# Stationary weights of an AdaLN mixture-of-experts feed-forward kernel stored in other forms

## The chip, the cores and the metric

The kernel runs on one core of one Trainium2 chip. The metric is device microseconds (us) from the start of the program to its end. Of the kernel before, two runs took 1309.41 and 1309.58 us, median 1309.49 us.

## The reference, cut to what matters

```python
B, S, D = (32, 256, 256); F, E, R, K = 1024, 8, 16, 2
# attention: q = x + bias of the sequence's stage, keys and values are the side input
attn = softmax(einsum('bsd,btd->bst', q, side));  o = einsum('bst,btd->bsd', attn, side)
# feed-forward with two of eight low-rank experts for each token
t = o * rsqrt(mean(o * o) + EPS) * norm_w
probs = softmax(t @ gate_w.T);  topw, topi = top_k(probs, K)
h1 = (t @ w1.T)[None] + SCALING * einsum('etr,efr->etf', einsum('td,erd->etr', t, a1), b1)
h3 = (t @ w3.T)[None] + SCALING * einsum('etr,efr->etf', einsum('td,erd->etr', t, a3), b3)
act = silu(h1) * h3
out_e = act @ w2.T + SCALING * einsum('etr,edr->etd', einsum('etf,erf->etr', act, a2), b2)
out = x + weighted sum of out_e over the token's two experts
```

## The kernel before, in words

All products are wanted in nearly float32 precision. Every operand is therefore stored as two tensors of the type float32r (a float32 that TensorE streams in one pass): a rounded high part `_hi`, and the rest, `_lo`. The helper `product` in the TensorE part makes one product out of three matmuls: high weight with high stream, high weight with low stream, low weight with high stream. In the profile these three are the lines L1201, L1202 and L1203, for every product of the kernel. For each matmul TensorE first loads a stationary operand of 128 columns (a row of the engine PEld), then streams the moving operand past it (a row of PE). A tile in the trace reads `bank<-t_hi,w1T_hi`: the moving operand is named first, the stationary one second.

The kernel has two phases. In the first, 32 sequences go through attention, one at a time; on TensorE there are 256-column products with q, k, prob and value, and 128-column transposes of q, kv and prob. Between them lie 21 "weight jobs" (the list `jobs`): a job transposes up to four 128x128 blocks of a weight into a PSUM bank (`weight_job`, L1247), ScalarE copies the bank into the high part (`weight_high`, L639), VectorE writes the low part (`weight_low`, L848). The weights of `w2` and `a2` arrive with the eight chunks interleaved, so the transposes of these jobs already load a stationary operand whose columns lie eight words (32 bytes) apart (`w2_in[:, c, j0 + k:F:FC]` and `a2_in[:, j0 + k:F:FC]`); those of `w1`, `w3` and `b` load packed columns.

In the second phase, 8192 tokens go through the feed-forward in 16 tiles of 512 tokens; in each tile a loop runs over 8 chunks j of 128 hidden features. `low_rank` multiplies with a13T; `first_expert` with w1T, b1T, w3T and b3T; `second_expert` with b1T and b3T; `down_z` with a2T. In all these the weight is stationary and 512 columns of tokens are streamed. `down_y` and `finish_y` are the other way round: the activation (s or z) is stationary and 256 columns of w2T or b2T are streamed. The order on TensorE is written out by hand in `pe_tile`. 

The stationary operand of a chunk is today a packed run of 128 words, 512 bytes. The allocations are laid out one behind the other, with pads: in the kernel before, all weights that are loaded as stationary, and t_hi, t_lo, v_hi, v_lo, s and br that are streamed or loaded in the second phase, start at the same place within a 512-byte grid (byte 384). The streamed kT, probT, w2T and b2T start at other places, by gaps of 8 to 88 words ahead of them.

Of the kernel before, what the change touches and what calls it, by code (L numbers as in the profile page):

```python
# [31 lines left out]
P = 128  # L32
# [20 lines left out]
def adaln_moe_ffn(nc, x, side, itok, embed, norm_w, w1, w3, w2, gate_w, a1, b1, a3, b3, a2, b2, out):  # L53
    ctx = ExitStack()
    with ctx:
# [6 lines left out]
        def sb(stack, name, shape, dt=F32):  # L62
            return stack.enter_context(nc.sbuf_tensor(name, shape, dt))
# [7 lines left out]

        sb(ctx, "pad_w", [P, 352])
        ident = sb(ctx, "ident", [P, P])
# [7 lines left out]

        w1T = split("w1T", [P, DC, F])
        w3T = split("w3T", [P, DC, F])
        w2T = split("w2T", [P, FC, D], gaps=(16, 24))
        a2T = split("a2T", [P, FC, ER], gaps=(88, 0))
# [35 lines left out]

        sb(ctx, "pad_t", [P, 48])
        O_STRIDE = P + 32
# [181 lines left out]
        for j0 in range(0, FC, 2):  # L305
            jobs.append(([(128 * (2 * k + c), 128, w2_in[:, c, j0 + k:F:FC], P)
                          for k in range(2) for c in range(DC)],
                         [(0, 512, w2T[0][:, j0:j0 + 2].rearrange("p j d -> p (j d)"),
                           w2T[1][:, j0:j0 + 2].rearrange("p j d -> p (j d)"), 1.0)]))
        B_JOB = len(jobs)  # L310
        for src, dst in ((b1_by_j, b1T), (b3_by_j, b3T)):
            for j0 in range(0, FC, 4):
                jobs.append(([(128 * k, 128, src[:, j0 + k].rearrange("p e r -> p (e r)"), P) for k in range(4)],
                             [(0, 512, dst[0][:, j0 * P:(j0 + 4) * P],
                               dst[1][:, j0 * P:(j0 + 4) * P], SCALING)]))
        A2_JOB = len(jobs)
        for j0 in range(0, FC, 4):
            jobs.append(([(128 * k, 128, a2_in[:, j0 + k:F:FC], ER) for k in range(4)],
                         [(0, 512, a2T[0][:, j0:j0 + 4].rearrange("p j e -> p (j e)"),
                           a2T[1][:, j0:j0 + 4].rearrange("p j e -> p (j e)"), 1.0)]))  # L320
        B2_JOB = len(jobs)
# [508 lines left out]
        def _(dve):  # L830
# [14 lines left out]
            def weight_low(n):  # L845
                dve.wait_ge(w_hi_ready, n + 1)
                for col, cols, hi, lo, scale in jobs[n][1]:
                    last = nc.vector.scalar_tensor_tensor(lo, job_bank(n)[:, col:col + cols], scale, f32(hi),  # L848
                                                          ALU.mult, ALU.subtract)
                last.then_inc(w_lo_ready, 1)  # L850
# [346 lines left out]
        def _(pe):  # L1197
# [188 lines left out]
            def first_expert(c, j):  # L1386
                f = slice(j * P, (j + 1) * P)
                for wT, bT, dst, k, done in ((w1T, b1T, h1_bank[j % 2], 0, h1_first),
                                             (w3T, b3T, h3_bank[j % 2], 1, h3_first)):
                    if j == 0:  # L1390
                        pe.wait_ge(v_ready, v_count(c, k + 2))
                    for dc in range(DC):
                        product(dst[:, :], at(wT, ALL, dc, f), (t_hi[c % 2][:, dc], t_lo[c % 2][:, dc]), dc == 0, False)
                    if j == 0:
                        pe.wait_ge(v_lo_ready, v_count(c, k))
                    product(dst[:, :], at(bT, ALL, f), (v_hi[k][:, :], v_lo[k][:, :]), False, True).then_inc(done, 1)

            def second_expert(c, j):
# [18 lines left out]
            def last_down_z(c, j):  # L1417
                (hi, lo), (s_high, s_low) = at(a2T, ALL, j), at(s_at(c, j), ALL, ALL)
                pe.wait_ge(last_br_ready, 1)
# [102 lines left out]
```

## Time and profile before

| | kernel before |
|---|---|
| median of the runs | 1309.49 us |
| the profiled execution, device time | 1309.57 us |
| its span from the first to the last instruction | 1307.7 us |
| TensorE matmul busy | 1300.9 us, 7278 instructions |
| TensorE weight load busy | 1138.8 us, 7278 instructions |
| VectorE, ScalarE, GpSimd busy | 844.1, 527.1, 250.0 us |
| granted TensorE clock | 1.000, all of the span |
| first phase, second phase | 0 to 179 us, 179 to 1307.7 us |

The profile is of one execution. Times in it are us, the mean duration of a group is ns. Matmul records overlap: the next one starts while the last one drains, and its end is modelled. How fast TensorE goes is read from start to start, in the timeline, and not from the durations. PE is a matmul, PEld a weight load. "x4" is four like instructions merged into one row.

### The profile page before, as it was taken

How to read it: one execution, taken by the hardware profiler on the slowest of the kernel's cores; microseconds unless marked ns; L12 is line 12 of the kernel's file. 1: busy time of each engine (PE TensorE's matmuls, PEld its weight loads, DVE VectorE, ACT ScalarE, POOL GpSimd, SP SyncE). 2: the span in 40 equal slices, each digit the busy share in tenths (PEclk: the TensorE clock that was granted, in tenths of full speed). 3: DMA queues.
4: the chain of work that ended last, by engine and by line, in shares of the span. 5: the costliest groups of instructions: out<-in, count | busy, mean ns of one | idle time of the engine just before them, and what ended most of it. 6: DMA issues, size and time to landing. Idle time of an engine off the chain costs nothing.

```text
span 1307.7 us, 18591 instructions
## 1 busy us (share of the span) xinstructions
PE 1300.9 (99%) x7278; PEld 1138.8 (87%) x7278; DVE 844.1 (65%) x1558; ACT 527.1 (40%) x991; POOL 250.0 (19%) x213
## 2 busy tenths in 40 slices
PE   9999999999999999999999999999999999999998
PEld 8999998888888888888888888888888888888887
DVE  6776656756666576656775567557675666565556
ACT  6776653333343334333333334333333343243332
POOL 2656640202011020202020202011020202020200
PEclk9999999999999999999999999999999999999999
DMA  9454811020202020101102020202020101102000
GB/s 287 140 159 147 233 50 33 2 73 1 73 2 73 1 73 1 58 17 28 46 2 73 1 73 2 73 1 73 2 73 1 57 17 34 41 1 73 1 17 17
DMA packets 73583, 69.56 MB, mean 53 GB/s; under 512 B 7050, under 2 KB 64792, under 8 KB 73368
## 3 DMA queue, kind: packets, MB, share of 16 engines
q1 hardware_dynamic: 72924, 68.11, 17.4%
q8 instruction: 57, 0.93, 0.3%
q10 hardware_dynamic: 572, 0.28, 0.1%
q14 instruction: 30, 0.25, 0.1%
HBM read 51.27 MB, written 17.10 MB: 52 GB/s over the span
## 4 chain that ended last, share of the span: by engine, by line
PE 98%; ACT 1%; DVE 1%; DMA 0%; issue 0%; ACTq 0%; DVEq 0%
PE bank L1202 31%; PE bank L1201 31%; PE bank L1203 31%; PE bank L1327 2%; PE bank L1254 2%; PE bank L1305 1%; PE bank L1247 1%; DMA kv<-in_fside_BxSxS 0%; ACT prob L662 0%; PE bank L1292 0%; ACT kT_hi L646 0%; ACT qT_hi L645 0%; DVE q L858 0%; DVE x_out L1145 0%; PE bank L1334 0%
## 5 line engine op out<-in xcount | busy, mean ns | idle before, releaser
L1073 DVE TENSOR_TENSOR act_a<-silu_a,bank 128x512 f32<-128x512 f32 x128 | 87.6, 685 | 211.2 <-PE bank L1203 194.6
L753 ACT ACTIVATE br_hi<-act_br 128x512 fp32r<-128x512 f32 x128 | 80.9, 632 | 188.5 <-DVE act_br L1084 188.5
L746 ACT ACTIVATE silu_b<-bank 128x512 f32<-128x512 f32 x128 | 76.2, 596 | 187.9 <-PE bank L1203 187.1
L589 POOL TENSOR_TENSOR t_lo<-t_in,t_hi 128x512 fp32r<-128x512 f32 x32 | 40.6, 1290 | 552.2 <-ACT t_hi L733 552.2
L1202 PE MATMUL bank<-w2T_lo,s_hi 128*128 128x256 f32 x512 | 144.7, 283 | 0.0
L1203 PE MATMUL bank<-w2T_hi,s_lo 128*128 128x256 f32 x512 | 143.3, 280 | 0.0
L1201 PE MATMUL bank<-w2T_hi,s_hi 128*128 128x256 f32 x512 | 142.7, 279 | 0.0
L1081 DVE TENSOR_TENSOR act_b<-silu_b,bank 128x512 f32<-128x512 f32 x128 | 87.9, 687 | 81.4 <-PE bank L1203 80.3
L742 ACT ACTIVATE silu_a<-bank 128x512 f32<-128x512 f32 x128 | 75.7, 591 | 134.3 <-PE bank L1203 134.2
L608 POOL TENSOR_TENSOR v_lo<-v_full,v_hi 128x512 fp32r<-128x512 f32 x64 | 94.5, 1511 | 136.7 <-ACT v_hi L738 136.7
L1094 DVE TENSOR_TENSOR br_lo<-act_br,br_hi 128x512 fp32r<-128x512 f32 x128 | 104.7, 818 | 5.6 <-ACT br_hi L753 3.1
L1088 DVE TENSOR_TENSOR act_s<-act_a,act_br 128x512 f32<-128x512 f32 x128 | 103.2, 806 | 4.4
L1201 PE MATMUL bank<-t_hi,w1T_hi 128*128 128x512 f32 x256 | 100.4, 392 | 0.0
L1084 DVE TENSOR_TENSOR act_br<-act_b,rho 128x512 f32<-128x512 f32 x128 | 97.2, 760 | 4.4
L1203 PE MATMUL bank<-t_hi,w1T_lo 128*128 128x512 f32 x256 | 99.9, 390 | 0.0
L1201 PE MATMUL bank<-v_hi,b1T_hi 128*128 128x512 f32 x256 | 99.8, 390 | 0.0
L1202 PE MATMUL bank<-t_lo,w1T_hi 128*128 128x512 f32 x256 | 99.7, 390 | 0.0
L1202 PE MATMUL bank<-v_lo,b1T_hi 128*128 128x512 f32 x256 | 99.7, 390 | 0.0
L1201 PE MATMUL bank<-v_hi,b3T_hi 128*128 128x512 f32 x256 | 99.7, 389 | 0.0
L1202 PE MATMUL bank<-v_lo,b3T_hi 128*128 128x512 f32 x256 | 99.6, 389 | 0.0
L1203 PE MATMUL bank<-v_hi,b1T_lo 128*128 128x512 f32 x256 | 99.6, 389 | 0.0
L1201 PE MATMUL bank<-t_hi,w3T_hi 128*128 128x512 f32 x256 | 99.6, 389 | 0.0
(197 smaller groups left out, 3242.4 us busy)
## 6 DMA issues: line engine op xcount, KB each, us to landing
x_in<-in_x SPq DMA_DIRECT2D x32, 256.0 KB, 3.7
t_scratch<-oT SPq DMA_DIRECT2D x32, 256.0 KB, 2.5
t_in<-t_scratch SPq DMA_DIRECT2D x16, 512.0 KB
x_out<-in_x SPq DMA_DIRECT2D x16, 512.0 KB, 3.9
kv<-in_fside_BxSxS SPq DMA_DIRECT2D x31, 256.0 KB, 3.4
out<-x_out SPq DMA_DIRECT2D x30, 256.0 KB, 4.0
rho<-scale_scratch SPq DMA_DIRECT2D x16, 256.0 KB
rstd<-scale_scratch SPq DMA_DIRECT2D x16, 256.0 KB
```

The source lines that it names most:

```text
L608: nc.gpsimd.tensor_tensor(v_lo[k][:, :], v_full[k][:, :], f32(v_hi[k][:, :]), ALU.subtract).then_inc(v_lo_ready, 1)
L742: nc.scalar.activation(silu_a[j % 2][:, :], h1_bank[j % 2][:, :], ACT.Silu).then_inc(silu_a_ready, 1)
L746: nc.scalar.activation(silu_b[:, :], h1_bank[j % 2][:, :], ACT.Silu).then_inc(silu_b_ready, 1)
L753: nc.scalar.activation(br_hi[j % 2][:, :], act_br[j % 2][:, :], ACT.Copy).then_inc(br_hi_ready, 1)
L1073: nc.vector.tensor_tensor(act_a[j % 2][:, :], silu_a[j % 2][:, :], h3_bank[j % 2][:, :], ALU.mult).then_inc(act_a_ready, 1)
L1081: nc.vector.tensor_tensor(act_b[:, :], silu_b[:, :], h3_bank[j % 2][:, :], ALU.mult).then_inc(act_b_ready, 1)
L1084: nc.vector.tensor_tensor(act_br[j % 2][:, :], act_b[:, :], rho[c % 2][:, :], ALU.mult).then_inc(act_br_ready, 1)
L1088: nc.vector.tensor_tensor(act_s[j % 2][:, :], act_a[j % 2][:, :], act_br[j % 2][:, :], ALU.add).then_inc(act_s_ready, 1)
L1094: low = nc.vector.tensor_tensor(br_lo[j % 2][:, :], act_br[j % 2][:, :], f32(br_hi[j % 2][:, :]), ALU.subtract)
L1201: nc.tensor.matmul(dst, w_hi, x_hi, start=start, stop=False, skip_group_check=not grouped)
L1202: nc.tensor.matmul(dst, w_hi, x_lo, start=False, stop=False, skip_group_check=not grouped)
L1203: return nc.tensor.matmul(dst, w_lo, x_hi, start=False, stop=stop, skip_group_check=not grouped)
```

## The change

The change stores the stationary weights of the second phase in other forms, and leaves every instruction of TensorE in its place, with its shape.

- w1T: the high and low parts are interleaved word by word in one tensor `w1T_pair`, so the columns of each lie 8 bytes apart.
- a2T: four chunks are interleaved; columns 16 bytes apart.
- b1T: eight chunks are interleaved; columns 32 bytes apart.
- w3T and b3T stay packed, but begin 16 and 8 bytes (w3T high, low), 4 and 12 bytes (b3T high, low) off the 32-byte grid.
- w2T, the streamed weight, keeps its 256 packed words for each chunk, with 8 words (32 bytes) of room behind each. The weight jobs of w2T then write two pieces of 256 columns where they wrote one of 512.
- Pads and gaps are changed so that all other tensors keep their place within the 512-byte grid.

```diff
+        w1T_pair = sb(ctx, "w1T_pair", [P, DC, F, 2], F32R)
+        w1T = tuple(w1T_pair[:, :, :, k] for k in range(2))
+        w3T_hi = moved("w3T_hi", 4, DC * F)
+        sb(ctx, "w3T_gap", [P, 120])
+        w3T_lo = moved("w3T_lo", 2, DC * F)
+        w3T = tuple(part.rearrange("p (c f) -> p c f", c=DC) for part in (w3T_hi, w3T_lo))
+        w2T_rows = split("w2T", [P, FC, D + 8], gaps=(8, 0))
+        w2T = tuple(part[:, :, 0:D] for part in w2T_rows)
+        a2T_rows = split("a2T", [P, FC // 4, ER, 4], gaps=(112, 0))
+        a2T = tuple(part[:, :, :, :].rearrange("p f e i -> p f i e") for part in a2T_rows)
         a13T = split("a13T", [P, DC, 2, ER])
-        b1T = split("b1T", [ER, F])
-        b3T = split("b3T", [ER, F])
-        b2T = split("b2T", [ER, D], gaps=(72, 32))
+        b1T_rows = split("b1T", [ER, P, FC])
+        b1T = tuple(part[:, :, :].rearrange("p c f -> p f c") for part in b1T_rows)
+        b3T_hi = moved("b3T_hi", 1, F)
+        sb(ctx, "b3T_gap", [P, 120])
+        b3T_lo = moved("b3T_lo", 3, F)
+        b3T = b3T_hi, b3T_lo
+        b2T = split("b2T", [ER, D], gaps=(64, 32))
...
-                         [(0, 512, w2T[0][:, j0:j0 + 2].rearrange("p j d -> p (j d)"),
-                           w2T[1][:, j0:j0 + 2].rearrange("p j d -> p (j d)"), 1.0)]))
+                         [(256 * k, 256, w2T[0][:, j0 + k], w2T[1][:, j0 + k], 1.0) for k in range(2)]))
...
-                    last = nc.scalar.activation(hi, job_bank(n)[:, col:col + cols], ACT.Copy, scale=scale)
+                    last = nc.scalar.activation(hi, shaped(job_bank(n)[:, col:col + cols], hi), ACT.Copy, scale=scale)
```

Here `moved(name, words, n)` takes a tensor of n + 8 words and gives n words of it, beginning `words` words in.

On TensorE the order is the same row for row. This is the start of `first_expert` in the first tile, where the first chunk is multiplied with w1T and b1T. Before:

```order
L1201 MATMUL bank<-t_hi,w1T_hi 128x512
L1202 MATMUL bank<-t_lo,w1T_hi 128x512
L1203 MATMUL bank<-t_hi,w1T_lo 128x512
L1201 MATMUL bank<-t_hi,w1T_hi 128x512
L1202 MATMUL bank<-t_lo,w1T_hi 128x512
L1203 MATMUL bank<-t_hi,w1T_lo 128x512
L1201 MATMUL bank<-v_hi,b1T_hi 128x512
```

And in the change, at the same place:

```order
L1217 MATMUL bank<-t_hi,w1T_pair 128x512
L1218 MATMUL bank<-t_lo,w1T_pair 128x512
L1219 MATMUL bank<-t_hi,w1T_pair 128x512
L1217 MATMUL bank<-t_hi,w1T_pair 128x512
L1218 MATMUL bank<-t_lo,w1T_pair 128x512
L1219 MATMUL bank<-t_hi,w1T_pair 128x512
L1217 MATMUL bank<-v_hi,b1T_hi 128x512
```

Nothing moved; the source lines are 16 further down, and high and low weight of w1T have one tensor's name.

On ScalarE, in the first phase, the four jobs of w2T stand between the copies of attention. Before:

```order
L646 ACTIVATE kT_hi<-bank 128x512
L639 ACTIVATE w2T_hi<-bank 128x512
L662 ACTIVATE prob,row_sum<-bank,neg_max 128x256 x2
L656 ACTIVATE value_hi<-kv 128x512
L675 ACTIVATE oT<-bank 128x4x128
```

In the change:

```order
L662 ACTIVATE kT_hi<-bank 128x512
L655 ACTIVATE w2T_hi<-bank 128x256 x2
L678 ACTIVATE prob,row_sum<-bank,neg_max 128x256 x2
L672 ACTIVATE value_hi<-kv 128x512
L691 ACTIVATE oT<-bank 128x4x128
```

One ACTIVATE of 512 columns has become two of 256, four times; the same holds for the low parts on VectorE. GpSimd and the DMA queue have the same rows as before.

## Rows read from the trace of the kernel before

**Rows 1.** The page: span, busy time of the engines, granted clock.
```profile
span 1307.7 us, 18591 instructions
PE 1300.9 (99%) x7278; PEld 1138.8 (87%) x7278; DVE 844.1 (65%) x1558; ACT 527.1 (40%) x991; POOL 250.0 (19%) x213
PEclk9999999999999999999999999999999999999999
```

**Rows 2.** The page: the chain that ended last, by engine.
```profile
PE 98%; ACT 1%; DVE 1%; DMA 0%; issue 0%; ACTq 0%; DVEq 0%
```

**Rows 3.** Windows: stretch, then PE, PEld, DVE, ACT, POOL busy, granted clock.
```profile
8.00:66.00 58.00, 56.59 (x476) 55.70 (x476) 43.08 (x101) 42.86 (x106) 28.73 (x31) 1.00 0.71 216
...
700.00:1280.00 580.00, 580.00 (x2994) 497.67 (x2994) 367.60 (x599) 205.09 (x345) 78.36 (x56) 1.00 0.10 30
```

**Rows 4.** Matmul groups by form: line, tile, shapes, count | busy us, mean ns.
```profile
L1202 PE MATMUL bank<-w2T_lo,s_hi 128*128 128x256 f32 x512 | 144.7, 283 | 0.0
...
L1201 PE MATMUL bank<-t_hi,w1T_hi 128*128 128x512 f32 x256 | 100.4, 392 | 0.0
...
L1201 PE MATMUL bank<-br_hi,a2T_hi 128*128 128x512 f32 x128 | 49.8, 389 | 0.0
...
L1202 PE MATMUL bank<-probT_lo,value_hi 128*128 128x256 f32 x128 | 35.9, 280 | 0.0
L1327 PE MATMUL bank<-oT 128*128 128x136 f32 x256 | 34.9, 279 | 0.0
```

**Rows 5.** Timeline of PE from 699.83 us: start, duration, line, tile.
```profile
699.83 0.28 PE L1202 MATMUL bank<-w2T_lo,s_hi 128*128 128x256 f32 x1
...
702.07 0.28 PE L1203 MATMUL bank<-w2T_hi,s_lo 128*128 128x256 f32 x1
...
704.50 0.39 PE L1202 MATMUL bank<-t_lo,w3T_hi 128*128 128x512 f32 x1
...
711.98 0.39 PE L1202 MATMUL bank<-t_lo,w3T_hi 128*128 128x512 f32 x1
```

**Rows 6.** Timeline of PEld, weight loads of the same stretch.
```profile
701.96 0.19 PEld L1203 LDWEIGHTS bank<-w2T_hi,s_lo 128*128 128x128 f32 x1
...
704.50 0.19 PEld L1203 LDWEIGHTS bank<-t_hi,w3T_lo 128*128 128x128 f32 x1
```

**Rows 7.** Weight load groups: count | busy us, mean ns.
```profile
L1201 PEld LDWEIGHTS bank<-v_hi,b1T_hi 128*128 128x128 f32 x256 | 48.1, 188 | 9.5
...
L1327 PEld LDWEIGHTS bank<-oT 128*128 128x128 f32 x256 | 32.0, 190 | 0.2
```

**Rows 8.** Timeline of PE in the first phase: transposes of packed and spaced columns, then oT.
```profile
34.25 0.60 PE L1254 MATMUL bank<-ident,kv 128*128 128x128 f32 x4
34.68 0.60 PE L1247 MATMUL bank<-ident,w_in 128*128 128x128 f32 x4
35.12 1.09 PE L1327 MATMUL bank<-oT 128*128 128x136 f32 x8
```

**Rows 9.** Weight loads of L1247: duration ns least, median, most; first and last start.
```profile
L1247 PEld LDWEIGHTS bank<-ident,w_in x48: 139/140/193, 11.5 to 44.1; 128*128 128x128 f32 x48
L1247 PEld LDWEIGHTS bank<-ident,a_in x12: 185/189/230, 6.7 to 62.0; 128*128 128x128 f32 x12
```

**Rows 10.** Timeline of weight loads: first a w3 job (packed), then a w2 job (spaced).
```profile
31.84 0.47 PEld L1247 LDWEIGHTS bank<-ident,w_in 128*128 128x128 f32 x4
...
34.58 0.51 PEld L1247 LDWEIGHTS bank<-ident,w_in 128*128 128x128 f32 x4
```

**Rows 11.** ScalarE's part of the weight jobs: duration ns least, median, most.
```profile
L639 ACT ACTIVATE w2T_hi<-bank x4: 605/622/646, 35.9 to 44.7; 128x512 fp32r<-128x512 f32 x4
...
L639 ACT ACTIVATE b2T_hi<-bank x1: 393/393/393, 65.7 to 65.7; 128x256 fp32r<-128x256 f32 x1
```

**Rows 12.** The same on VectorE.
```profile
L848 DVE SCALAR_TENSOR_TENSOR w2T_lo<-bank,w2T_hi x4: 679/680/681, 36.7 to 45.5; 128x512 fp32r<-128x512 f32 x4
...
L848 DVE SCALAR_TENSOR_TENSOR b2T_lo<-bank,b2T_hi x1: 412/412/412, 66.5 to 66.5; 128x256 fp32r<-128x256 f32 x1
```

More of the change, by code:

```diff
@@ L80, in split, with moved @@
             return tuple(parts)
[L82 to L85, printed above, removed]
-        a13T = split("a13T", [P, DC, 2, ER])
-        b1T = split("b1T", [ER, F])
-        b3T = split("b3T", [ER, F])
-        b2T = split("b2T", [ER, D], gaps=(72, 32))
+        def moved(name, words, n):
+            room = sb(ctx, name, [P, n + 8], F32R)
+            return room[:, words:words + n]
+        w1T_pair = sb(ctx, "w1T_pair", [P, DC, F, 2], F32R)
[8 more added lines that the diff above has]
+        a2T = tuple(part[:, :, :, :].rearrange("p f e i -> p f i e") for part in a2T_rows)
+        a13T = split("a13T", [P, DC, 2, ER])
+        b1T_rows = split("b1T", [ER, P, FC])
[5 more added lines that the diff above has]
+        b2T = split("b2T", [ER, D], gaps=(64, 32))
         sb(ctx, "pad_b2T", [P, 24])
@@ L312, in adaln_moe_ffn @@
             for j0 in range(0, FC, 4):
-                jobs.append(([(128 * k, 128, src[:, j0 + k].rearrange("p e r -> p (e r)"), P) for k in range(4)],
-                             [(0, 512, dst[0][:, j0 * P:(j0 + 4) * P],
-                               dst[1][:, j0 * P:(j0 + 4) * P], SCALING)]))
+                places = ([(0, 512, dst[0][:, j0:j0 + 4], dst[1][:, j0:j0 + 4], SCALING)]
+                          if dst is b1T else [(0, 512, dst[0][:, j0 * P:(j0 + 4) * P],
+                                               dst[1][:, j0 * P:(j0 + 4) * P], SCALING)])
+                jobs.append(([(128 * k, 128, src[:, j0 + k].rearrange("p e r -> p (e r)"), P) for k in range(4)], places))
         A2_JOB = len(jobs)
@@ L318, in adaln_moe_ffn @@
             jobs.append(([(128 * k, 128, a2_in[:, j0 + k:F:FC], ER) for k in range(4)],
[L319 to L320 removed]
+                         [(0, 512, a2T[0][:, j0 // 4], a2T[1][:, j0 // 4], 1.0)]))
         B2_JOB = len(jobs)
@@ L847, in weight_low @@
                 for col, cols, hi, lo, scale in jobs[n][1]:
-                    last = nc.vector.scalar_tensor_tensor(lo, job_bank(n)[:, col:col + cols], scale, f32(hi),
+                    last = nc.vector.scalar_tensor_tensor(lo, shaped(job_bank(n)[:, col:col + cols], lo), scale, f32(hi),
                                                           ALU.mult, ALU.subtract)
@@ L1395, in first_expert @@
                         pe.wait_ge(v_lo_ready, v_count(c, k))
-                    product(dst[:, :], at(bT, ALL, f), (v_hi[k][:, :], v_lo[k][:, :]), False, True).then_inc(done, 1)
+                    product(dst[:, :], at(bT, ALL, j if bT is b1T else f), (v_hi[k][:, :], v_lo[k][:, :]), False, True).then_inc(done, 1)
             def second_expert(c, j):
@@ L1417, in last_down_z @@
             def last_down_z(c, j):
-                (hi, lo), (s_high, s_low) = at(a2T, ALL, j), at(s_at(c, j), ALL, ALL)
+                (hi, lo), (s_high, s_low) = at(a2T, ALL, j // 4, j % 4), at(s_at(c, j), ALL, ALL)
                 pe.wait_ge(last_br_ready, 1)
```

12 lines of the change are left out of this document (7 added, 5 removed).

## The prediction

> **What bounds the kernel now.** I read the page first. TensorE's matmuls are busy for 1300.9 of 1307.7 us, the granted clock is at its upper level (2.4 GHz) in every slice [rows 1], and 98% of the chain that ended last lies on TensorE [rows 2]. In the second phase there is no gap in it at all: 580.00 of 580.00 us, with VectorE at 63% and ScalarE at 35% [rows 3]. So only what changes the pace of TensorE's stream counts.
>
> Busy time does not show that pace, since matmul records overlap; start-to-start times do. From the matmul at 704.50 us to the one at 711.98 us there are 33 steps of 512 columns, all with a new weight: 7.48 / 33 = 0.2267 us each [rows 5]. The stream alone, 512 columns at 2.4 GHz, would take 0.2133 us. Each 512-column matmul thus costs 13.4 ns more than its stream. The 256-column matmuls from 699.83 to 702.07 us are 19 steps in 2.24 us, 0.118 us each against 0.107 us of stream: 11 ns more [rows 5]. The excess goes with the matmul, not with its length.
>
> How much room has the weight load? It starts together with the matmul before its own: load and matmul both at 704.50 us [rows 5, 6]. Its record is 188 ns long [rows 7]. In the 256-column stretch the load for the matmul at 702.07 starts at 701.96 us, yet that matmul starts 0.11 us later, though the record runs to 702.15 [rows 5, 6]. So the last 70 ns or so of a record hold nobody up, and a load needs at most 118 ns of its engine. In the 512-column stretch there are 227 ns. The slack is at least 227 - 118 = 109 ns for each load.
>
> **The change, part by part.** The profiled execution took 1309.57 us, of which 1307.7 are the span and 1.9 lie around it; the median of the runs is 1309.49, the same within 0.1 us.
>
> *Columns 8, 16, 32 bytes apart (w1T, a2T, b1T).* Each pair of a high and a low weight makes three matmuls: 3 x 256 with w1T, 3 x 256 with b1T, 6 x 128 with a2T [rows 4, 7], 768 for each of the three and 2304 together. What does a spaced load cost? The trace has them: the transposes of the w2 and a2 jobs load columns 32 bytes apart. Packed, such a load takes 140 ns (the median of all w_in), spaced up to 193, and a2's a_in have a median of 189 [rows 9]; four in a row take 0.51 instead of 0.47 us [rows 10]. So spacing costs a transpose's load about 50 ns. An ordinary load takes 188 ns packed [rows 7], as much as a spaced transpose load. I see two bounds. Below: 0, if the 188 ns is already the pace of one column at a time, which spacing doesn't alter; I take this one, since 187 to 193 ns and 188 ns are the same pace. Above: +53 ns, to 241 ns. Of that bound 118 + 53 = 171 ns count, still under 227. Either way the load stays hidden under the matmul before it, and the cost is 2304 x 0 = 0. The cover would be gone only if a load's own part grew past 227 ns, almost twice its 118.
>
> *w3T and b3T, 4 to 16 bytes off the grid.* These are 2 x 768 = 1536 loads under 512-column streams, and they stay packed. No row shows such a start; the nearest is that of packed loads, 188 ns [rows 7]. A run of 128 words that begins off the grid can touch at most one piece more of the memory than on it, 1 part in 32 of 118 ns, 4 ns, against a slack of 109. Cost 0.
>
> *w2T, 32 bytes further from chunk to chunk.* This is a streamed operand, and its 1536 matmuls of 256 columns run at 0.118 us [rows 4, 5]. Now each chunk begins at another place in the 512-byte grid. The trace of before has several such places: w2T_lo, 283 ns, and probT_lo, 280 ns, start 40 and 32 to 112 words off the stationary grid and last the same within 3 ns [rows 4]. I take 0, and 3 ns x 1536 = 4.6 us either way as bounds.
>
> *Jobs of the first phase.* ScalarE writes w2T_hi in two pieces: 2 x 393 instead of 622 ns, +0.16 us for each of four jobs [rows 11]; VectorE 2 x 412 instead of 680, +0.14 [rows 12]. Uncovered that is 4 x 0.30 = 1.2 us. It is covered: from 8 to 66 us ScalarE and VectorE have 15 us free each, and TensorE waits 1.4 us in all [rows 3]. Eight jobs (w1T, b1T, a2T) now write with spaced columns. No row prices that. If it doubled ScalarE's and VectorE's part (0.62 + 0.68 us) and nothing covered it, it would be 8 x 1.3 = 10 us; since both engines have room for all of it, I take 0, and 2 us as the upper bound.
>
> Sum: 1309.5 + 0 + 0 + 0 + 0 = about 1310 us, with a range of its own of 1303 to 1317.
>
> The Trainium skill, in "SBUF — State Buffer", section "Door 1: The DMA port swizzle", says that memory lines are 16 bytes, that two accesses to a line are needed for full bandwidth and that each step to a new line pays a penalty. By that w1T would be free, and b1T and a2T would not. The trace bears out that spacing costs a transpose's load something. If the penalty stays under the slack, the page and my sum give the same time; the two rivals that follow are what it gives if not.
>
> **Rival 1, slower: a load's reads take turns from the stream.** The 13.4 ns are 32 periods of 2.4 GHz, and 32 is a quarter of the load's 128 columns: as if each four packed columns stopped the stream once. Speaking for it: the eight oT matmuls stream 136 columns at half the pace (113.3 ns) with the same 190 ns loads [rows 7], and go (1.09 - 0.28) / 7 = 0.116 us from start to start [rows 8], only 2.7 ns over their stream. Where the stream leaves every second turn free, the load disturbs it little; where it takes every turn, 13.4 ns. Against it: the excess could as well belong to each column loaded, or be a fixed price of changing weights at full pace. The spaced transposes cannot decide, since their stream leaves turns free too: a w2 job goes from 34.68 to 35.12 us, 0.44 us, the packed kv before it from 34.25 to 34.68, 0.43 [rows 8]. If it holds, columns 8 bytes apart stop the stream 64 times (+13.3 ns), 16 and 32 bytes apart 128 times (+40 ns each): 768 x (13.3 + 40 + 40) = 71.7 us, 1381 us. It decides as soon as an additional stop costs more than a third of what it does today.
>
> The Trainium skill speaks against this rival: "TensorE: Matmul & The Clock Gate", section "Step-by-step: what each phase is for", says that the stream and the weight load have independent read ports and that loading steals no read bandwidth from a running matmul.
>
> **Rival 2: spaced loads become longer than their cover.** Doubling the 118 ns for a2T and b1T gives 236, 9 ns over 227: 1536 x 9 = 14 us, 1324 us, within 2%. Tripling gives 354, 127 ns over: 195 us, 1505 us. Against it: the 193 ns of rows 9.
>
> **Rival 3, faster: the spacing keeps load and stream out of each other's way.** If the 13.4 ns come from both readers meeting in the same part of the memory, a load with 8 bytes a column walks at another pace than today, and may meet the stream less. Down to the 2.7 ns of oT that gives 10.7 ns a matmul: for the 2304 spaced ones 24.7 us, 1285 us; with w3T and b3T (3840 in all) 41 us, 1268 us. Against it: the excess is 11 to 13 ns wherever the streams begin.
>
> **How the numbers follow.** The forecast gets 0.50. Rival 1 gets 0.20, as the oT rows are good evidence for half of it. Rival 2 gets 0.12, half within 2% and half beyond. Rival 3 gets 0.18, 0.11 of it beyond 2%, if the off-grid weights gain as well or the gain per matmul is larger. About 2% is what a measurement of this kernel can tell from no change. Faster 0.11, same 0.50 + 0.06 + 0.07 = 0.63, slower 0.20 + 0.06 = 0.26. The range from 1284 to 1382 us leaves out 0.11 below and 0.06 above.
>
> **What the profile would show.** Right: steps of 0.227 us between 512-column matmuls for all weights, loads of 188 to 241 ns, 580.00 busy of 580. Rival 1: 0.240 us after the start of a matmul during which a w1T weight is loaded, 0.267 for a2T and b1T, w3T and b3T as before. Rival 2: loads of a2T and b1T near 300 ns and TensorE paced by them. Rival 3: steps below 0.227 us. Gaps of TensorE between 30 and 66 us would show my cover for the jobs wrong.

## The result, and the profile after

The change takes 1341.69 us (1340.58 and 1342.81, median of two), before 1309.49. The ratio is 1.0248, with a 95% interval of 1.0231 to 1.0264: 32.2 us slower. That is within the stated range of 1284 to 1382 us, but 32 us off the likeliest case and outside the 1303 to 1317 us of the sum itself. The range reached this far for the sake of rival 1, whose sizes turned out wrong; that the time fell inside is owed to the width of the range and not to the sum.

| | before | after |
|---|---|---|
| median of the runs | 1309.49 us | 1341.69 us |
| span of the profiled execution | 1307.7 us | 1341.0 us |
| weight load busy | 1138.8 us | 1223.2 us |
| first phase ends | 179.1 us | 181.2 us |
| mean step after a 512-column matmul, second phase | 227.3 ns | 235.0 ns |
| mean step after a 256-column matmul, second phase | 118.2 ns | 118.3 ns |

The steps are my count over all matmuls of the second phase, from the start of one to the start of the next. 4032 steps of 512 columns, each 7.7 ns longer, are 31.0 us. The profiled execution is the longer of the two, 33.2 us over the profiled one of before (1342.81 against 1309.57 us); nearly all the rest is a first phase that ends 2.1 us later. Of the page of the profile, which [rows 1, 2] show of before:

```profile
span 1341.0 us, 18599 instructions
PE 1332.1 (99%) x7278; PEld 1223.2 (91%) x7278; DVE 846.8 (63%) x1562; ACT 532.0 (40%) x995; POOL 250.0 (19%) x213
...
PE 96%; ACT 2%; DMA 1%; DVE 1%; SPq 0%; issue 0%; DVEq 0%
```

TensorE's share says nothing: 99% before and after. The windows (stretch; then PE, PEld, DVE, ACT, POOL busy; granted clock), to be held against [rows 3]:

```profile
8.00:66.00 58.00, 54.53 (x457) 52.26 (x458) 43.04 (x102) 43.94 (x106) 27.72 (x30) 1.00 0.67 207
700.00:1280.00 580.00, 580.00 (x2913) 527.06 (x2912) 360.70 (x589) 201.52 (x337) 78.33 (x56) 1.00 0.11 34
```

In the second phase TensorE is still busy for 580.00 of 580.00 us at the full clock (its upper level, 2.4 GHz), but gets 2913 matmuls done where it did 2994. The weight loads fill 527 us of it instead of 498. The load groups (count | busy us, mean ns of one | idle of the load unit just before them), to be held against 188 ns and 9.5 us of idle time in [rows 7]:

```profile
L1218 PEld LDWEIGHTS bank<-v_lo,b1T_hi 128*128 128x128 f32 x256 | 84.8, 331 | 0.0
L1219 PEld LDWEIGHTS bank<-v_hi,b1T_lo 128*128 128x128 f32 x256 | 84.2, 329 | 0.0
...
L1217 PEld LDWEIGHTS bank<-t_hi,w1T_pair 128*128 128x128 f32 x256 | 49.7, 194 | 5.8
...
L1217 PEld LDWEIGHTS bank<-t_hi,w3T_hi 128*128 128x128 f32 x256 | 49.0, 191 | 5.4
...
L1219 PEld LDWEIGHTS bank<-t_hi,w3T_lo 128*128 128x128 f32 x256 | 48.0, 188 | 11.1
L1218 PEld LDWEIGHTS bank<-br_lo,a2T_hi 128*128 128x128 f32 x128 | 39.6, 310 | 0.0
```

Three kinds stand here. Columns 8 bytes apart cost a load 6 ns. Columns 16 and 32 bytes apart cost it 121 to 143 ns, and within a series its unit has no idle time left ahead of it. (Records of over 0.3 us that start every 0.24 us overlap, so an idle time of 0.0 does not yet say that a matmul waited.) The off-grid w3T stays at 188 to 191.

Next, PE's timeline, first and last matmul of each run of steps (start, duration), and the weight loads of the same stretch:

```profile
705.81 0.53 PE L1217 MATMUL bank<-v_hi,b1T_hi 128*128 128x512 f32 x1
706.18 0.40 PE L1218 MATMUL bank<-v_lo,b1T_hi 128*128 128x512 f32 x1
...
707.12 0.39 PE L1219 MATMUL bank<-v_hi,b3T_lo 128*128 128x512 f32 x1
...
708.53 0.39 PE L1219 MATMUL bank<-br_hi,a2T_lo 128*128 128x512 f32 x1
...
709.92 0.40 PE L1219 MATMUL bank<-t_hi,w1T_pair 128*128 128x512 f32 x1
...
710.64 0.40 PE L1219 MATMUL bank<-v_hi,b1T_lo 128*128 128x512 f32 x1
...
712.03 0.40 PE L1219 MATMUL bank<-t_hi,w3T_lo 128*128 128x512 f32 x1
```

```profile
705.70 0.32 PEld L1217 LDWEIGHTS bank<-v_hi,b1T_hi 128*128 128x128 f32 x1
...
709.92 0.32 PEld L1217 LDWEIGHTS bank<-v_hi,b1T_hi 128*128 128x128 f32 x1
710.16 0.33 PEld L1218 LDWEIGHTS bank<-v_lo,b1T_hi 128*128 128x128 f32 x1
710.40 0.33 PEld L1219 LDWEIGHTS bank<-v_hi,b1T_lo 128*128 128x128 f32 x1
710.65 0.19 PEld L1217 LDWEIGHTS bank<-t_hi,w3T_hi 128*128 128x128 f32 x1
```

Read against the 0.2267 us of [rows 5], all with 512 columns:

- six steps from 707.12 to 708.53 us, a2T being loaded: 0.235 us each;
- six from 708.53 to 709.92, w1T loaded: 0.232;
- three from 709.92 to 710.64, b1T loaded: 0.240. The loads follow each other at 0.24, 0.24 and 0.25 us as well. Each starts with a matmul, so these times alone do not tell which of the two waits for the other;
- six from 710.64 to 712.03, w3T loaded: 0.232, although these loads are as short as before.

At 705.81 a step takes 0.37 us. The b1T load of 0.32 us starts at 705.70 under a 256-column matmul, which covers only 0.12 of it. There are 15 such steps, one for each tile behind `finish_y`: 15 x (0.367 - 0.227) = 2.1 us.

These steps show that a long load does hold TensorE up, and where the wait is booked. The record of the matmul begins at 705.81 us, before its own load ends at 706.02, and is 0.53 us long: the wait stands in the step that begins with the matmul that uses the load. They also give an estimate of the part of a load that holds TensorE up: cover plus long step less a stream, 0.116 + 0.367 - 0.227, about 255 ns for the first load of b1T here. In the kernels below with b1T alone, the same 15 steps are 361 ns at 32 bytes and 343 ns at 16 (counted in their traces), which gives 255 and 235 ns.

By weight loaded, over the whole second phase: the mean step in ns, without the steps over 0.3 us. "Loaded" is the weight whose load starts with the step, which the next matmul uses. The experiments of the last seven columns follow below: b1T 8, 16, 32 bytes apart; a2T 16; the off-grid w3T and b3T; the same two packed at other places; and the change with b1T packed.

| loaded | before | change | b1 8 B | b1 16 B | b1 32 B | a2 16 B | off-grid | places | change, b1T packed |
|---|---|---|---|---|---|---|---|---|---|
| w1T high, low | 228.4, 227.5 | 232.0, 233.1 | 228.4, 227.5 | 228.4, 227.5 | 228.4, 227.5 | 229.0, 232.5 | 228.9, 228.3 | 229.2, 228.3 | 232.4, 233.0 |
| a2T high | 226.7 | 234.4 | 226.7 | 228.6 | 227.9 | 234.8 | 231.9 | 227.4 | 236.8 |
| a2T low | 226.7 | 235.1 | 226.7 | 229.3 | 230.0 | 235.8 | 228.1 | 227.9 | 234.3 |
| b1T high | 227.4 | 240.3 | 232.0 | 235.2 | 237.7 | 226.8 | 229.4 | 228.9 | 231.2 |
| b1T low | 227.3 | 245.4 | 233.2 | 233.2 | 248.1 | 227.2 | 230.5 | 228.8 | 230.5 |
| w3T high | 226.7 | 233.4 | 229.2 | 230.5 | 232.9 | 226.7 | 229.0 | 232.1 | 228.9 |
| w3T low | 226.7 | 227.5 | 226.7 | 233.3 | 233.6 | 226.7 | 227.1 | 228.8 | 227.1 |
| b3T high | 226.9 | 234.5 | 229.2 | 229.3 | 233.3 | 226.9 | 232.3 | 231.7 | 232.3 |
| b3T low | 226.9 | 231.7 | 226.7 | 231.3 | 232.3 | 226.9 | 229.4 | 231.2 | 229.4 |

High weights are loaded about 512 times, low ones 256. The additions for the change are therefore, in us: w1T 3.1, a2T 6.0, b1T 10.9 and the 2.1 of the 15 long steps, w3T 3.7, b3T 5.1; together 30.9. The rows of w3T and b3T are the surprise: 8.8 us with loads of 188 to 192 ns. A small part of it is b1T's, since the wait for its last load stands one step further on. Counted by the weight that the step's own matmul uses, the same trace gives w1T 3.7, a2T 6.0, b1T 14.2 (the long steps included), w3T 2.8 and b3T 4.5 us: 7.3 of the 8.8 us stay with w3T and b3T.

The weight jobs, to be held against [rows 11, 12] (duration least, median, most; first and last start):

```profile
L655 ACT ACTIVATE w2T_hi<-bank x8: 390/423/451, 37.0 to 46.2; 128x256 fp32r<-128x256 f32 x8
L655 ACT ACTIVATE w1T_pair<-bank,nw x4: 725/742/772, 14.2 to 19.8; 128x512 fp32r<-128x512 f32 x4
L655 ACT ACTIVATE w3T_hi<-bank,nw x4: 696/715/732, 22.9 to 33.9; 128x512 fp32r<-128x512 f32 x4
...
L655 ACT ACTIVATE b1T_hi<-bank x2: 1197/1222/1247, 49.1 to 52.4; 128x512 fp32r<-128x512 f32 x2
L655 ACT ACTIVATE b3T_hi<-bank x2: 610/628/645, 55.5 to 58.4; 128x512 fp32r<-128x512 f32 x2
L655 ACT ACTIVATE a2T_hi<-bank x2: 1117/1134/1152, 61.5 to 64.7; 128x512 fp32r<-128x512 f32 x2
```

```profile
L864 DVE SCALAR_TENSOR_TENSOR b1T_lo<-bank,b1T_hi x2: 1123/1136/1148, 50.3 to 53.7; 128x512 fp32r<-128x512 f32 x2
L864 DVE SCALAR_TENSOR_TENSOR b3T_lo<-bank,b3T_hi x2: 681/682/683, 56.5 to 59.1; 128x512 fp32r<-128x512 f32 x2
L864 DVE SCALAR_TENSOR_TENSOR a2T_lo<-bank,a2T_hi x2: 1108/1113/1118, 62.6 to 65.9; 128x512 fp32r<-128x512 f32 x2
```

Writes 8 bytes apart are nearly free (742 against 715 ns). Those 16 and 32 bytes apart take nearly double: b1T 1222 against 628 for the packed b3T, and 1136 against 682 on VectorE, which also reads the spaced high part.

TensorE is busy 54.53 of the 58 us of this stretch, 56.59 before. Of these 2.1 us, 1.6 lie before 30 us, where TensorE waits mostly for data to arrive (0.89 us for kv, 0.59 for w_in) and for q. Between 30 and 66 us, where the prediction wanted to see no gap, TensorE is busy for 35.57 of 36.00 us, before for all 36.00: the cover of the jobs leaks 0.4 us. In the last three kernels below, which keep at least six of the eight spaced jobs, that leak is 0.2 to 0.4 us and the second phase begins between 179.0 and 179.3 us; one of them keeps all eight and the split w2T jobs too, and begins it at 179.0. So I don't count the later start of this one execution as a cost of the change.

### The profile page after: what moved, and what is told of

Same layout as the page of the kernel before. It is cut to its first block, busy times and chain, and to the rows that moved or that the text cites. A ratio compares the mean times of both kernels' runs of the same rounds, so it can differ in the third digit from the quotient of the medians.

```text
span 1341.0 us, 18599 instructions
## 1 busy us (share of the span) xinstructions
PE 1332.1 (99%) x7278; PEld 1223.2 (91%) x7278; DVE 846.8 (63%) x1562; ACT 532.0 (40%) x995; POOL 250.0 (19%) x213
## 4 chain that ended last, share of the span: by engine, by line
PE 96%; ACT 2%; DMA 1%; DVE 1%; SPq 0%; issue 0%; DVEq 0%
PE bank L1217 30%; PE bank L1219 30%; PE bank L1218 30%; PE bank L1270 2%; PE bank L1343 2%; PE bank L1321 1%; ACT prob L678 1%; DMA x_in<-in_x 0%; DMA kv<-in_fside_BxSxS 0%; PE bank L1263 0%; ACT qT_hi L661 0%; ACT kT_hi L662 0%; DVE q L874 0%; SPq L411 0%; SPq L460 0%
## 5 line engine op out<-in xcount | busy, mean ns | idle before, releaser
L1217 PE MATMUL bank<-v_hi,b1T_hi 128*128 128x512 f32 x256 | 106.1, 415 | 0.0
L1218 PE MATMUL bank<-v_lo,b1T_hi 128*128 128x512 f32 x256 | 104.7, 409 | 0.0
L1219 PE MATMUL bank<-v_hi,b1T_lo 128*128 128x512 f32 x256 | 102.9, 402 | 0.0
L1219 PE MATMUL bank<-v_hi,b3T_lo 128*128 128x512 f32 x256 | 101.6, 397 | 0.0
L1219 PE MATMUL bank<-t_hi,w1T_pair 128*128 128x512 f32 x256 | 101.2, 395 | 0.0
L1219 PE MATMUL bank<-t_hi,w3T_lo 128*128 128x512 f32 x256 | 101.0, 394 | 0.0
L1217 PE MATMUL bank<-t_hi,w1T_pair 128*128 128x512 f32 x256 | 100.8, 394 | 0.0
L1218 PE MATMUL bank<-t_lo,w1T_pair 128*128 128x512 f32 x256 | 100.8, 394 | 0.0
```

The lines of the kernel that those rows point to most:

```text
L1217: nc.tensor.matmul(dst, w_hi, x_hi, start=start, stop=False, skip_group_check=not grouped)
L1218: nc.tensor.matmul(dst, w_hi, x_lo, start=False, stop=False, skip_group_check=not grouped)
L1219: return nc.tensor.matmul(dst, w_lo, x_hi, start=False, stop=stop, skip_group_check=not grouped)
```

## The experiments

Two theories are weighed. One is that of cover: a spaced load grows longer than the matmul above it, and only then costs. The other is that of disturbance: a load disturbs the running stream by how or where it reads, though it is itself in time. Every ratio is against the kernel before, run on the same chip. The source lines shift by some rows from kernel to kernel.

### w1T alone, 8 bytes apart

```diff
-        w1T = split("w1T", [P, DC, F])
+        w1T_pair = sb(ctx, "w1T_pair", [P, DC, F, 2], F32R)
+        w1T = tuple(w1T_pair[:, :, :, k] for k in range(2))
```

> Only w1T has its columns 8 bytes apart; all else is the kernel before. Theory A (a load that is spaced too far becomes long, and TensorE waits for it where the matmul before it does not cover it): in the changed kernel w1T's loads took 194 ns against 188, so they stay covered; time 1309 to 1311 us, and steps of about 227 to 228 ns. Theory B (a load's reads take turns from the stream, by the number of pieces of memory that it touches): twice the pieces, +5 to +13 ns for each of the 768 matmuls under which w1T is loaded, +4 to +10 us, 1314 to 1320 us, with the load's record no longer than before.

Measured: 1313.72 against 1308.97 us, ratio 1.0034 [1.0022, 1.0047], +4.8 us. One load group, and PE's timeline with six steps ahead of which w1T is loaded:

```profile
L1202 PEld LDWEIGHTS bank<-t_hi,w1T_pair 128*128 128x128 f32 x256 | 49.7, 194 | 8.7
```

```profile
710.60 0.39 PE L1204 MATMUL bank<-br_hi,a2T_lo 128*128 128x512 f32 x1
...
712.00 0.40 PE L1204 MATMUL bank<-t_hi,w1T_pair 128*128 128x512 f32 x1
```

The load is 6 ns longer and has idle time ahead of it (8.7 us over 256), yet each of the six steps takes 0.233 us, 6 ns more. The load is not late. Cover alone can't explain this; the result lies between the two expectations. In this form w1T high still begins at its old place and w1T low 4 bytes behind it, and both have mean steps of 233 ns (232.7 and 232.9), so it is the spacing that costs here and not those 4 bytes.

### a2T alone, 16 bytes apart

```diff
-        a2T = split("a2T", [P, FC, ER], gaps=(88, 0))
+        a2T_rows = split("a2T", [P, FC // 4, ER, 4], gaps=(88, 0))
+        a2T = tuple(part[:, :, :, :].rearrange("p f e i -> p f i e") for part in a2T_rows)
```

> Only a2T has its columns 16 bytes apart. In the changed kernel its loads took 309 ns against 188. Theory A: the load's own part is about 118 + 121 = 239 ns, 12 ns over the 227 of its cover, for 768 loads, +9 us, 1318 us; the steps are all near 239 ns, set by the load. Theory B: stops of the stream that come on top of its own pace, +40 ns by the count of pieces, +31 us, 1340 us. The sum by weight in the changed kernel's trace gave +6 us for a2T; I expect 1315 to 1319 us.

Measured: 1317.50 against 1308.97 us, 1.0064 [1.0049, 1.0079], +8.5 us.

```profile
L1205 PEld LDWEIGHTS bank<-br_lo,a2T_hi 128*128 128x128 f32 x128 | 39.6, 309 | 0.0
```

The load goes from 188 to 309 ns, with no idle time left. By the arithmetic of the prediction its own part is 118 + 121 = 239 ns, 12 over the 227 of the stream; the steps are 231 to 240 ns long, mean 235 to 236. In the mean, cover says what happens, and the 235 ns from the long steps above agree. It does not say it step by step: the six steps of a series are 231, 240, 232, 238, 231 and 240 ns, where the expectation had all of them near 239. And 1.3 us of the loss lies in steps under which the untouched w1T low is loaded (232.5 instead of 227.5 ns).

### b1T alone, 32 bytes apart

```diff
-        b1T = split("b1T", [ER, F])
+        b1T_rows = split("b1T", [ER, P, FC])
+        b1T = tuple(part[:, :, :].rearrange("p c f -> p f c") for part in b1T_rows)
```

> Only b1T has its columns 32 bytes apart. In the changed kernel its loads took 317 to 331 ns. Theory A: its own part is about 118 + 135 = 253 ns, up to 26 ns over the cover, less where a stop of the stream isn't needed: +11 to +20 us for 768 loads, and once a tile, behind the 256-column matmuls of finish_y, a step of 367 ns in which the cover is only 118 ns (15 times, 2 us); 1322 to 1331 us. Theory B: +31 us, 1340 us, the same as for a2T, since both touch one piece for each column.

Measured: 1332.85 against 1308.97 us, 1.0180 [1.0165, 1.0195], +23.9 us. Load group, then PE's timeline:

```profile
L1208 PEld LDWEIGHTS bank<-v_hi,b1T_lo 128*128 128x128 f32 x256 | 85.2, 333 | 0.0
```

```profile
704.39 0.40 PE L1208 MATMUL bank<-t_hi,w1T_lo 128*128 128x512 f32 x1
...
705.11 0.41 PE L1208 MATMUL bank<-v_hi,b1T_lo 128*128 128x512 f32 x1
...
705.83 0.39 PE L1208 MATMUL bank<-t_hi,w3T_lo 128*128 128x512 f32 x1
...
706.51 0.39 PE L1208 MATMUL bank<-t_hi,w3T_lo 128*128 128x512 f32 x1
...
707.19 0.40 PE L1208 MATMUL bank<-v_hi,b3T_lo 128*128 128x512 f32 x1
```

The three steps from 704.39 with b1T loaded take 0.240 us. Then the first three with the *unchanged* w3T loaded take 0.240 each as well (249, 236 and 235 ns), and from 705.83 on the steps are back at 0.227. The 249 ns are still the wait for the last load of b1T, booked one step on; the two behind it are slow although the loads are 188 to 192 ns long. So something is handed on. How far differs from place to place: over the 128 times that w3T follows b1T, its six steps have means of 243, 235, 236, 226, 229 and 231 ns. With columns 16 bytes apart the trail is longer and even: 230, 231, 236, 228, 232 and 231 ns behind b1T, 224, 231, 236, 228, 232 and 231 behind a2T, and then 227. Nor does the load ahead have to be late: in the kernel with w1T alone the two steps behind w1T's 194 ns loads are 233 and 231 ns, with packed b1T loaded. By the table, 4.9 + 4.7 = 9.6 of the 23.9 us lie in the steps of w3T and b3T; counted by the weight that the step's own matmul uses, 5.8.

### w3T and b3T alone, 4 to 16 bytes off the grid

```diff
-        w3T = split("w3T", [P, DC, F])
+        w3T_hi = moved("w3T_hi", 4, DC * F)
+        sb(ctx, "w3T_gap", [P, 120])
+        w3T_lo = moved("w3T_lo", 2, DC * F)
...
+        b3T_hi = moved("b3T_hi", 1, F)
+        sb(ctx, "b3T_gap", [P, 120])
+        b3T_lo = moved("b3T_lo", 3, F)
```

> Only w3T (16 and 8 bytes) and b3T (4 and 12 bytes) are off the 32-byte grid. In the changed kernel the steps while these were loaded were 227.5 to 234 ns, which may be delay handed on from the long loads of b1T and a2T, or their own. If it is handed on (theory A alone): 1309 to 1311 us and steps of 227 ns. If a start off the grid, or a start at another place than the stream's, itself costs something: +3 to +7 ns for 1536 loads, +5 to +9 us, 1314 to 1319 us, and then by load: w3T low (8 bytes) nothing, the other three 4 to 6 ns.

Measured: 1319.30 against 1308.97 us, 1.0078 [1.0063, 1.0093], +10.3 us, with loads like this:

```profile
L1213 PEld LDWEIGHTS bank<-t_hi,w3T_hi 128*128 128x128 f32 x256 | 48.1, 188 | 10.2
```

The load records are unchanged within 1 ns, and yet 10 us. This is disturbance without any lack of cover. The time is at the upper end of the second expectation, but its sizes by load are not borne out: w3T high rises by 2.3 ns, w3T low by 0.4, b3T high by 5.4 and b3T low by 2.5. Over half of the loss lies in the steps of weights that were not touched, a2T high (231.9 ns) and b1T (229.4 and 230.5) above all.

### b1T 8 bytes apart, and 16

```diff
+        b1T_pair = sb(ctx, "b1T_pair", [ER, FC, P, 2], F32R)
+        b1T = tuple(b1T_pair[:, :, :, k] for k in range(2))
```

> Only b1T is changed, to columns 8 bytes apart (high and low word by word, as w1T is in the change). w1T alone with 8 bytes cost 4.8 us for 768 loads (steps of 233 ns), with loads of 194 ns. If the price goes with the spacing and not with the weight: +4 to +7 us, 1313 to 1316 us, loads of 194 ns, and no 367 ns steps behind finish_y. If b1T is dear for its place in the order, whatever its spacing: over +12 us.

```diff
+        b1T_rows = split("b1T", [ER, FC // 4, P, 4])
+        b1T = tuple(part[:, :, :, :].rearrange("p a c i -> p a i c") for part in b1T_rows)
```

> Only b1T is changed, to columns 16 bytes apart, as a2T is in the change. a2T alone with 16 bytes cost 8.5 us (loads 309 ns), b1T alone with 32 bytes 23.9 us (loads 317 to 342 ns). If the length of the load decides: loads of 309 ns, steps of 230 to 240 ns, +8 to +12 us with about 2 us of it behind finish_y, 1317 to 1321 us. If one piece of memory for each column is what costs, 16 and 32 bytes are the same: about +24 us, 1333 us.

Measured, against 1309.28 us: 8 bytes apart 1315.04, 1.0043 [1.0027, 1.0059], +5.8; 16 bytes apart 1324.32, 1.0113 [1.0095, 1.0131], +15.0. A load group of the kernel with 8 bytes:

```profile
L1206 PEld LDWEIGHTS bank<-v_hi,b1T_pair 128*128 128x128 f32 x256 | 49.7, 194 | 9.4
```

And one of the kernel with 16:

```profile
L1207 PEld LDWEIGHTS bank<-v_lo,b1T_hi 128*128 128x128 f32 x256 | 79.6, 311 | 0.0
```

With one weight, the loads are 188 ns packed, 194 at 8 bytes, up to 311 at 16, up to 333 at 32. The jump lies between 8 and 16. The Trainium skill, "SBUF — State Buffer", section "Door 1: The DMA port swizzle", has memory lines of 16 bytes, with two accesses to a line for the full rate and a penalty for each new line; the trace agrees for weight loads on where the jump lies, with these four numbers. By that rule 16 and 32 bytes, both with one column to a line, would be alike; the further 22 ns are not in it. The 15 long steps are there at 16 bytes (0.343 us) and at 32 (0.361) and not at 8 (0.234). The whole program pays 0, 5.8, 15.0 and 23.9 us. The 5.8 are as expected; the 15.0 lie above the one expectation and below the other. Nor does the length of the load decide alone: a2T with the same 16 bytes and the same 309 ns cost 8.5 us. b1T is loaded in 256 groups of three, a2T in 128 groups of six, and behind a group come the six slow steps seen above; in the trace with b1T 16 bytes apart 7.6 us lie in the steps of the untouched w3T, b3T and a2T.

### w3T and b3T packed, on the 32-byte grid, at other places

Compared with the kernel before, w3T high and low are moved by 32 and 64 bytes, b3T high and low by 128 and 256; all four remain multiples of 32 bytes.

```diff
+        w3T_hi = moved("w3T_hi", 8, DC * F)
+        w3T_lo = moved("w3T_lo", 16, DC * F)
...
+        b3T_hi = moved("b3T_hi", 32, F)
+        b3T_lo = moved("b3T_lo", 64, F)
```

> The kernel before, with w3T and b3T packed and on the 32-byte grid, but off their place within 512 bytes: w3T high by 32, low by 64 bytes, b3T high by 128, low by 256. The off-grid kernel (4 to 16 bytes) cost 10.3 us. If it is the start inside a 32-byte piece that costs: this one is 1309 us with steps of 227 ns. If it is any shift of the load against the stream (the streams start at byte 384 as the weights did): +5 to +15 us, 1314 to 1324 us, with steps while w3T and b3T are loaded that differ by the size of the shift.

Measured: 1318.11 against 1309.02 us, 1.0069 [1.0053, 1.0086], +9.1 us. Load group, and seven matmuls between the first and the last of which w3T is loaded six times:

```profile
L1213 PEld LDWEIGHTS bank<-t_hi,w3T_hi 128*128 128x128 f32 x256 | 48.1, 188 | 10.8
```

```profile
707.36 0.40 PE L1215 MATMUL bank<-v_hi,b1T_lo 128*128 128x512 f32 x1
...
708.75 0.39 PE L1215 MATMUL bank<-t_hi,w3T_lo 128*128 128x512 f32 x1
```

1.39 / 6 = 0.232 us. The program loses about as much as off the grid. So a start off the 32-byte grid is not needed; it is enough that the weight no longer begins at the place in the 512-byte grid that it shared with the streams and with the other weights. The steps do not follow the size of the shift: 232.1 ns at 32 bytes, 228.8 at 64, 231.7 at 128, 231.2 at 256. Whether the place counts against the streams or against the weights loaded just before and behind is not separated: no run here moves the streams alone by other than whole 512 bytes.

### All activations 1024 bytes further

```diff
-            sb(ctx, "pad_t", [P, 48])
+            sb(ctx, "pad_t", [P, 304])
```

> Nothing but the pad ahead of the activations is changed: all streamed tensors of the second phase lie 1024 bytes further on, as they do in the changed kernel and in the kernel with off-grid weights, all weights stay. Their places within 512 bytes are the same. In the off-grid kernel the steps during which the untouched a2T and b1T are loaded rose to 228 to 235 ns. If that is from these 1024 bytes: +3 to +5 us, 1312 to 1314 us, with the same steps. If only the place within 512 bytes counts: 1309 us and 227 ns, and the rise was handed on from the off-grid loads.

Measured: 1309.17 against 1309.28 us, 0.9998 [0.9989, 1.0008]. 1024 bytes leave their place in the 512-byte grid as it is. The off-grid kernel had moved its activations by 1024 bytes as a side effect, and this kernel excludes that as the cause. (Its other side effect, ident and w1T 1024 bytes lower, was not run by itself.) PE's timeline:

```profile
701.83 0.40 PE L1201 MATMUL bank<-t_hi,w1T_hi 128*128 128x512 f32 x1
...
703.23 0.39 PE L1201 MATMUL bank<-v_hi,b1T_hi 128*128 128x512 f32 x1
...
703.68 0.39 PE L1203 MATMUL bank<-v_hi,b1T_lo 128*128 128x512 f32 x1
...
711.84 0.39 PE L1203 MATMUL bank<-t_hi,w3T_lo 128*128 128x512 f32 x1
```

From 703.68 to 711.84 us there are 36 steps of 0.2267 us, as in [rows 5]. The first six, from 701.83, directly behind the 256-column matmuls, take 0.233 us each, and the kernel before has the same six (702.19 to 703.59 us in its timeline). Even an all-packed kernel thus knows two paces, and falls into the faster one after a few matmuls. The kernel before stays in it, with 3603 of its 4032 steps at 226 or 227 ns; the changed one is thrown out of it again and again, and has 202.

### The low part of w2T at another place

```diff
-        w2T = split("w2T", [P, FC, D], gaps=(16, 24))
-        a2T = split("a2T", [P, FC, ER], gaps=(88, 0))
+        w2T = split("w2T", [P, FC, D], gaps=(16, 64))
+        a2T = split("a2T", [P, FC, ER], gaps=(48, 0))
```

a2T's gap only takes back what w2T's adds.

> Nothing is spaced. Only the gaps ahead of w2T are other: w2T low begins 40 words further on, at byte 192 of the 512-byte grid instead of 32, w2T high stays at 448. In the changed kernel this pair of places is that of chunk 0, whose 256-column steps were 113.3 ns, all of them, where those of the other chunks and of the kernel before are 117 to 120. If the place of the streamed weight against the loaded one decides: all 1536 steps at 113.3 ns instead of 117.8, -7 us, 1302 us, and up to 2 us more if the 512-column steps behind them, 229 to 239 ns now, fall to 227. If chunk 0 is fast for another reason (its turn in the order): 1309 us.

Measured: 1309.14 against 1309.28 us, 0.9998 [0.9988, 1.0008]. In the change the w2T steps of chunk 0 take 113.3 ns, others up to 119.8, with a mean of 117.8 as before. I had hoped to get the 113.3 by giving w2T low that chunk's place. The steps of chunk 0 stayed at 118.1 ns. The traces of the last three kernels below narrow it down: 113.3 ns are there too without the off-grid part, and 117.8 without b1T's spacing or without w2T's rooms, so it takes both of these. What makes the 113.3 stays open.

### The change without one of its parts

Without the b1T part (b1T packed again):

```diff
-        b1T_rows = split("b1T", [ER, P, FC])
-        b1T = tuple(part[:, :, :].rearrange("p c f -> p f c") for part in b1T_rows)
+        b1T = split("b1T", [ER, F])
```

> The changed kernel with b1T packed as before. One by one the parts cost 4.8 (w1T), 8.5 (a2T), 23.9 (b1T) and 10.3 us (off the grid), 47.5 us, but the change cost 32.2. If they share costs, because the loads of b1T hand a delay on to those of w3T and b3T, which in the kernel with b1T alone took 9.8 us of the 23.9: taking b1T out gives back only about 10 to 15 us, 1327 to 1332 us. If they are independent and something else in the change (w2T's rows) gains 15 us: it gives back 24 us, 1318 us.

Without the off-grid part:

```diff
-        w3T_hi = moved("w3T_hi", 4, DC * F)
-        w3T_lo = moved("w3T_lo", 2, DC * F)
+        w3T = split("w3T", [P, DC, F])
...
-        b3T_hi = moved("b3T_hi", 1, F)
-        b3T_lo = moved("b3T_lo", 3, F)
+        b3T = split("b3T", [ER, F])
```

> The changed kernel with w3T and b3T on the grid as before. If off-grid loads and the delay handed on by b1T and a2T are one and the same cost: 0 to -4 us, 1338 to 1342 us. If independent: -10 us, 1331 us.

Without the room between the chunks of w2T:

```diff
-        w2T_rows = split("w2T", [P, FC, D + 8], gaps=(8, 0))
-        w2T = tuple(part[:, :, 0:D] for part in w2T_rows)
+        w2T = split("w2T", [P, FC, D], gaps=(8, 24))
```

> The changed kernel with w2T packed as before, one piece for each job. The mean 256-column step of w2T was 117.8 ns before and 117.8 after, so I expect no difference, 1340 to 1343 us. If w2T's rows hide a gain of up to 15 us (the sum of the single parts is that much over the change), this one is at up to 1357 us.

Measured, against 1309.02 us:

| kernel | us | ratio | over before |
|---|---|---|---|
| change without b1T's spacing | 1328.41 | 1.0147 [1.0131, 1.0162] | +19.4 |
| change without the off-grid part | 1340.05 | 1.0236 [1.0220, 1.0251] | +31.0 |
| change without w2T's rooms | 1341.74 | 1.0247 [1.0232, 1.0263] | +32.7 |

The parts don't add. Alone they cost 4.8 + 8.5 + 23.9 + 10.3 = 47.5 us, together 32.2. Taking b1T's spacing away gives back about 13 us and not 24, and taking the off-grid part away under 2 and not 10. The table says why: behind b1T's late loads the steps of w3T and b3T are already slow (b1 32 B: 232 to 234 ns), and a weight off its place costs little more (change: 227.5 to 234.5). The kernel without the off-grid part shows it directly: w3T and b3T lie packed at their old places, and the steps with them loaded still take 8.6 us more than before, against 8.8 in the change. The last row prices w2T's rooms and its split jobs at nothing.

## Where the prediction was right and where it was wrong

**What bounds the kernel: right.** The second phase is TensorE's pace and nothing else; 31.0 of the 33.2 us of the profiled execution are longer 512-column steps. The steps of 256 columns stayed (118.2 to 118.3 ns).

**The price of a spaced load: wrong, and the main error.** I took 0 for it, because an ordinary load of 188 ns looked like the spaced transpose load of 187 to 193 ns, and +53 ns as the upper bound. Measured are +6 ns at 8 bytes, +121 at 16 and up to +145 at 32. The transpose's load gained 50 ns by spacing; that number doesn't carry over to an ordinary load, and equal durations were no sign of an equal pace. The upper bound was thus no bound. 118 + 121 = 239 and 118 + 143 = 261 ns exceed the 227 of cover. The 118 ns and with them the slack of 109 ns hold, since the 15 long steps give 235 and 255 ns for the first load of b1T.

**Rival 2 is the mechanism, in part.** Its signs are there: loads of 309 to 331 ns, idle 0.0 ahead of them, load after load at the step's length. Its price of 14 us for a2T and b1T at a doubling stands against 6.0 + 13.0 = 19 us in the steps of those two. The lateness is shown by the 15 long steps; that it is also what lengthens the other steps of b1T and a2T is argued from their means (235 ns at 16 bytes), beside a disturbance that acts at the same time.

**"w3T and b3T: cost 0": the second wrong step.** Loads of 188 to 192 ns stay far inside the slack, and their steps lengthen all the same, for 8.8 us in the change and 10.3 us in the off-grid kernel as a whole. The same holds for w1T: 3.1 us. The slack argument asks only whether a load is late. It leaves out that a load in time can slow the stream, and that this depends on where it begins and how it is spaced, and on what was loaded before it.

The Trainium skill, "TensorE: Matmul & The Clock Gate", section "Step-by-step: what each phase is for", has loading steal no read bandwidth from a running matmul. Here the runs disagree in the effect: packed loads of 188 ns at other places make 0.232 us of 0.227. They do not show in which port or memory the slowing arises.

**Rival 1: a true idea with wrong sizes.** The stream is disturbed by loads. But 13.3 ns for 8 bytes apart was 4 to 6 ns. 40 ns for both 16 and 32 was 8 ns for a2T, and 13 (high) and 18 (low) for b1T. Nor do the steps of w3T and b3T stay as before, as it wants. One stop per piece read would make 16 and 32 bytes equal; b1T's 15.0 and 23.9 us are not.

**Rival 3: no gain anywhere.** Its premise, that the places of loads matter to the stream, turned out true with the sign reversed. The kernel before has all stationary weights and streams at the same place in the 512-byte grid, and no weight's mean step in any run lies under 226.6 ns. "The excess is 11 to 13 ns wherever the streams begin" rested on streams of 256 columns, and was no evidence for those of 512.

**w2T: right.** 0, as forecast, within the 4.6 us (the last of the three kernels above).

**The jobs: right in the sum.** The two pieces take 423 ns each, forecast 393; the spaced writes double for four of the eight jobs, as the upper bound had it, and the cover holds but for 0.2 to 0.4 us, so the sign of being wrong that the prediction named, gaps between 30 and 66 us, did show, within the upper bound of 2 us. With all the jobs (the change without its off-grid part) the second phase still begins at 179.0 us, as before.

What stays open: why the stream slows when a packed load leaves the common place, and whether its place against the stream or against the other loads decides; why slow steps are handed on (two behind loads 8 bytes apart, about six behind loads 16 bytes apart); and the 113.3 ns of w2T's chunk 0. The runs show where and how much, not how.

## What to carry to other kernels

Keep a stationary operand packed where TensorE streams without a gap: columns 8 bytes apart cost little, from 16 bytes on the record of a load grows to 1.6 to 1.8 times its length and the part that holds TensorE up doubles, past even a 512-column matmul. Price a form that the trace lacks by a run of it alone, not by a like-looking duration of another instruction; and read start-to-start steps also for the weights that you did not touch, since part of the cost stands there. Costs of placement don't add up: undoing one of several bad forms may give back almost nothing.

## What the runs showed that I had not expected

- A weight load of 128 columns takes 188 ns packed, 194 at 8 bytes, 308 to 311 at 16, 317 to 333 at 32. Transposes' loads go only from 140 to 193 at 32 bytes.
- A stream of 512 columns has more than one pace with loads that are all in time: 226.7 ns a step, or 230 to 234. Moving two packed weights by 32 to 256 bytes away from the common place costs 9.1 us, moving all activations by 1024 bytes, two whole steps of the 512-byte grid, nothing.
- Slow steps are handed on to packed loads at their old places: two behind loads 8 bytes apart, six behind loads 16 bytes apart, two to six behind loads 32 bytes apart.
- ScalarE writes float32r 16 or 32 bytes apart at about half the rate (1134 and 1222 ns) and 8 bytes apart nearly as packed (742 ns). VectorE, which also reads the spaced high part, takes 1113 and 1136 ns where packed parts take 682.
